# Five conditioning vectors formed behind the expert slots, and the last head group's sum gated a step ahead

## The reference, cut to what matters

```python
mod = (silu(L_c) @ L_wmod).reshape(4, 6, 1, 512)      # one product of 4 x 512 by 512 x 3072
sa, ca, ga, sb, cb, gb = mod[:, 0], ..., mod[:, 5]
ga = sign(ga) * max(|ga|, 0.25);  gb = sign(gb) * max(|gb|, 0.25)
h = layernorm(x) * (1 + ca) + sa
x = x + ga * attn(h)
h = layernorm(x) * (1 + cb) + sb
x = x + gb * ffn(h)
```

## Time and profile before

| | |
|---|---|
| median of 3 runs | 1901.08 us (1898.94 to 1903.13) |
| the profiled execution | 1899.2 us, its span 1897.2 us |
| busy, TensorE (PE) | 1793.4 us, 95% |
| busy, TensorE's weight loads (PEld) | 1402.9 us, 74% |
| busy, VectorE (DVE) | 1179.9 us, 62% |
| busy, ScalarE (ACT) | 753.7 us, 40% |
| busy, GpSimd (POOL) | 682.8 us, 36% |
| DMA | 216.33 MB, 114 GB/s mean |
| chain that ended last | TensorE 76%, VectorE 10%, DMA 5%, GpSimd 3%, ScalarE 2% |

### The profile page before, as it was taken

How to read it: one execution, slowest core, us unless ns; L and a number is a source line. 1 busy time by engine, 2 the same in 40 slices (tenths; PEclk the granted TensorE clock), 3 DMA queues, 4 the chain that set the end, 5 groups by cost and what they waited for, 6 DMA issues and landing times.

```text
span 1897.2 us, 25664 instructions
## 1 busy us (share of the span) xinstructions
PE 1793.4 (95%) x8308; PEld 1402.9 (74%) x8308; DVE 1179.9 (62%) x2156; ACT 753.7 (40%) x1465; POOL 682.8 (36%) x674
## 2 busy tenths in 40 slices
PE   8889999999999999997897999949999999999998
PEld 4556788888888888885664777738778788788786
DVE  4555766666766666767773444466655747567576
ACT  2533455455455554543451222256642122212211
POOL 1334321222121121202153555634565445536332
PEclk9999999999999999999997999969999999999999
DMA  6122253635355454532267899740111011001001
GB/s 249 46 89 86 87 166 103 200 101 191 84 156 154 144 166 129 152 96 98 73 227 267 243 278 270 148 133 12 34 34 50 7 34 50 19 20 50 11 29 72
DMA packets 99953, 216.33 MB, mean 114 GB/s; under 512 B 8504, under 2 KB 33096, under 8 KB 98336
## 3 DMA queue, kind: packets, MB, share of 16 engines
q1 hardware_dynamic: 77744, 166.60, 27.5%
q0 software_dynamic: 11520, 28.96, 6.6%
q10 hardware_dynamic: 10608, 19.74, 3.2%
HBM read 123.93 MB, written 91.35 MB: 113 GB/s over the span
## 4 chain that ended last, share of the span: by engine, by line
PE 76%; DVE 10%; DMA 5%; issue 4%; POOL 3%; ACT 2%; POOLq 0%; ACTq 0%; DVEq 0%; SPq 0%
PE bank L781 21%; PE bank L783 20%; PE bank L782 20%; DMA u_d<-yt,sm 3%; PE bank L1167 3%; PE bank L1022 3%; PE bank L885 2%; PE bank L968 2%; DVE hh L2252 1%; POOL hs_d L2426 1%; DVE rr L1921 1%; PE bank L970 1%; PE bank L826 1%; PE bank L1168 1%; DMA gbt<-mod_rows_d,sm 1%
## 5 line engine op out<-in xcount | busy, mean ns | idle before, releaser
L1921 DVE RECIPROCAL rr<-rr 128x256 f32<-128x256 f32 x128 | 218.8, 1730 | 0.0
L781 PE MATMUL bank<-W1a,hT 128*128 128x512 f32 x512 | 209.9, 410 | 3.4 <-DVE hT L1833 3.4
L781 PE MATMUL bank<-hT,W1b 128*128 128x512 f32 x512 | 208.1, 406 | 2.6 <-DVE hh L2209 2.6
L782 PE MATMUL bank<-hT,W1b 128*128 128x512 f32 x512 | 203.3, 397 | 0.0
L783 PE MATMUL bank<-hT,W1b 128*128 128x512 f32 x512 | 203.2, 397 | 0.0
L783 PE MATMUL bank<-W1a,hT 128*128 128x512 f32 x512 | 201.5, 393 | 0.0
L782 PE MATMUL bank<-W1a,hT 128*128 128x512 f32 x512 | 200.7, 392 | 0.0
L2342 POOL TENSOR_TENSOR x<-x,tmp 128x512 f32<-128x512 f32 x60 | 95.9, 1598 | 245.9 <-DVE tmp L1913 245.9
L2209 DVE TENSOR_TENSOR hh<-hh,bank 128x512 f32<-128x512 f32 x64 | 43.7, 687 | 183.8 <-PE bank L783 147.3
L1946 DVE SCALAR_TENSOR_TENSOR kt<-bank,kt 128x256 fp32r<-128x256 f32 x128 | 50.7, 396 | 162.5 <-ACT vt L1388 162.3
L2276 POOL TENSOR_TENSOR W<-stage,W 128x1024 fp32r<-128x1024 f32 x32 | 77.2, 2412 | 184.4 <-ACT W L1250 182.1
(11 more groups left out here) (280 smaller groups left out, 4468.1 us busy)
## 6 DMA issues: line engine op xcount, KB each, us to landing
hs_d<-bor SPq DMA_DIRECT2D x24, 1548.0 KB, 11.7
ws_d<-W SPq DMA_DIRECT2D x48, 512.0 KB, 6.1
WB<-ws_d SPq DMA_DIRECT2D x8, 3072.0 KB, 18.8
stage<-wa SPq DMA_DIRECT2D x32, 512.0 KB, 5.2
stage<-wbe SPq DMA_DIRECT2D x24, 512.0 KB, 4.2
stage<-wdn SPq DMA_DIRECT2D x24, 512.0 KB, 3.9
mw<-wmod SPq DMA_DIRECT2D x10, 1024.0 KB, 4.9
hg<-hs_d ACTq DMA_DIRECT2D x39, 258.0 KB, 4.7
```

What stands on the lines that cost most here:

```text
L781: pe.matmul(o, lhs(HI), rhs(HI), start=start, stop=False, **kw)
L782: pe.matmul(o, lhs(HI), rhs(LO), start=False, stop=False, **kw)
L1921: dve.reciprocal(rr[:, pair, h], rr[:, pair, h]).then_inc(r_rec, 1)
```

## The change

It has two halves.

**The five late parts.** Five parts of layer 1 (SA, CA, SB, CB, GBT) are taken out of the tables of group 0, and so out of `mod_load`, `mod_products`, `mod_evac` and `mod_out`. They are made behind the expert slots instead:

- SyncE loads their weights (five times 1 MB, into a buffer `lw` of their own) at the end of `slots()`; the second and the fourth load wait for the end of the sixth and the seventh expert.
- TensorE makes the five products and four turns at the start of `back()`, into banks 0, 1, 4, 5 and 7, ahead of the transposes of the layernorm of batch 0.
- ScalarE copies rows and columns (`late_row`, `late_modc`) between and behind its diagonals, ahead of `ln_scaled(2, 0)`. `ln_scaled(2, 1)` goes behind `ln_out((2, 0))`.
- GpSimd makes the gate of GBT, and its transfer to `rows_d`, at the end of `step_c(0)` (`late_gate`).

**The last group's sum.** GpSimd multiplies `x` by the gate row and adds `x0` for a whole batch (`begin_gated`, eight operations), a step ahead of the batch's last tail. The tail is then one VectorE operation, PSUM times `row` into `tmp`, and GpSimd's add of `tmp` to `x`. The loads of `x0` for batches 2 and 3 stand in step (7,2), behind the counts that say where their buffers are free.

```diff
-MOD_PARTS = [(0, GAT), (0, SB), (0, CB), (0, GBT), (1, GAT), (1, SA), (1, CA), (1, SB), (1, CB), (1, GBT)]
-MOD_FINISH = [(0,), (3,), (4,), (9,)]
-MOD_PLACE = [(0, 0), (0, 1), (0, 2), (1, 0), (1, 2), (2, 0), (2, 1), (2, 2), (3, 0), (3, 2)]
+MOD_PARTS = [(0, GAT), (0, SB), (0, CB), (0, GBT), (1, GAT)]
+MOD_FINISH = [(0,), (3,), (4,), ()]
+MOD_PLACE = [(0, 0), (0, 1), (0, 2), (1, 0), (1, 2)]
+LATE_PARTS, LATE_ROW, LATE_BANK = [SA, CA, SB, CB, GBT], [0, 1, 2, 3, 1], [0, 1, 4, 5, 7]
@@ SyncE, called for i = 0 to 4 at the end of slots() @@
+            def late_load(i):
+                if i in (1, 3):
+                    e = (GE - 3, GE - 2)[i // 2]
+                    end = sp.value_load(tab[0:1, TAB_END, e:e + 1], min_val=1, max_val=SLOTS)
+                    sp.wait_ge(w_all, 16 * GE)
+                    sp.wait_ge(dn_full, end)
+                sp.dma_start(lw[:, i, :], wmod1[LATE_PARTS[i]]).then_inc(lw_loaded[i], 16)
@@ SyncE, load_x_again(b) @@
-                    sp.wait_ge(ring_done, RING[("tail", "A", GA - 1, {2: 0, 3: 2}[b])] + NT)
+                    sp.wait_ge(x_pre, NT * (b if b == 3 else 1))
                 sp.dma_start(x0[:, X0_AT[b], :, :], x_in[b].rearrange("(t p) n -> p t n", p=P)) \
@@ TensorE @@
             def back():
+                for i in range(3):
+                    late_product(i)
+                late_columns(0)
+                late_product(3)
+                late_columns(1)
+                late_product(4)
+                late_columns(2)
+                late_columns(3)
                 for half in range(2):
                     ln_transposes((2, 0), half)
@@ ScalarE, back() @@
                     for c in range(NC):
                         act.activation(dg[:, b, HI, c, :], ident[:, :], ACT.Copy, scale=gcol[:, c, b:b + 1]) \
                             .then_inc(dg_hi, 1)
+                    if b < 3:
+                        late_row(b)
+                late_modc(0)
+                late_row(3)
+                late_modc(1)
+                late_row(4)
+                late_modc(2)
+                late_modc(3)
                 ln_scaled(2, 0)
-                ln_scaled(2, 1)
                 ln_out((2, 0), 0)
                 ln_out((2, 0), 1)
+                ln_scaled(2, 1)
@@ VectorE, tail_evac @@
-                if ts == "A":
-
-                    link(dve.tensor_tensor(tmp[:, par, :], TAIL[par][:, :], xt, ALU.add), sum_done, tb * NT + t + 1)
-                    dve.tensor_tensor(tmp[:, par, :], tmp[:, par, :], row[:, tb % 2, :], ALU.mult) \
-                        .then_inc(ring_read, 1)
-                else:
-                    dve.tensor_tensor(tmp[:, par, :], TAIL[par][:, :], row[:, tb % 2, :], ALU.mult) \
-                        .then_inc(ring_read, 1)
+                dve.tensor_tensor(tmp[:, par, :], TAIL[par][:, :], row[:, tb % 2, :], ALU.mult).then_inc(ring_read, 1)
@@ GpSimd @@
+            def begin_gated(b):
+                pool.wait_ge(ring_read, RING[("tail", "A", GA - 2, b)] + NT)
+                pool.wait_ge(row_full[b % 2], 16 * (b // 2 + 1))
+                for t in range(NT):
+                    xt = x[:, b * NT + t, :]
+                    gated = pool.tensor_tensor(xt, xt, row[:, b % 2, :], ALU.mult)
+                    gated.then_inc(x_mul, 1)
+                pool.wait_ge(x_mul, NT * (b + 1))
+                pool.wait_ge(x0_loaded[X0_AT[b]], X0_COUNT[b])
+                for t in range(NT):
+                    xt = x[:, b * NT + t, :]
+                    pool.tensor_tensor(xt, xt, x0[:, X0_AT[b], t, :], ALU.add).then_inc(x_pre, 1)
@@ GpSimd, add_tail @@
-                    if ts == "A":
-                        pool.wait_ge(x0_loaded[X0_AT[tb]], X0_COUNT[tb])
-                        pool.tensor_tensor(xt, x0[:, X0_AT[tb], t, :], tmp[:, (key + t) % 2, :], ALU.add) \
-                            .then_inc(ring_done, 1)
-                        continue
                     pool.tensor_tensor(xt, xt, tmp[:, (key + t) % 2, :], ALU.add).then_inc(ring_done, 1)
@@ GpSimd, called at the end of step_c(0) @@
+            def late_gate():
+                v = prow[:, LATE_ROW[4], :]
+                pool.wait_ge(lm_row, len(LATE_PARTS))
+                gate(v)
+                pool.dma_start(rows_d[R_GB1], v).then_inc(row_stored[R_GB1], 16)
@@ GpSimd, step_a, ahead of the tail @@
+                if last and b > 0:
+                    begin_gated(b)
@@ GpSimd, step_a, at its end @@
+                if last and b == 0:
+                    begin_gated(0)
```

More of the change, by code:

```diff
@@ L437, in build @@
         nw_loaded = sem("norm_w_loaded")
+        lw_loaded = [sem(f"late_part_loaded{i}") for i in range(len(LATE_PARTS))]
+        lm_full = sem("late_part_full")
+        lm_row = sem("late_part_row_copied")
+        lc_full = sem("late_columns_full")
+        lc_done = sem("late_columns_copied")
         gw_loaded = sem("router_weights_loaded")
@@ L663, in step_a @@
                         wa_slice(1, 1)
-                    for i in ((1, 2, 3), (4, 5), (6, 7, 8), (9,))[b]:
+                    for i in ((1, 2, 3), (4,), (), ())[b]:
                         mod_load(i)
@@ L721, in slots @@
                     load_expert(e)
+                for i in range(len(LATE_PARTS)):
+                    late_load(i)
             def back():
```

58 lines of the change are left out of this document (41 added, 17 removed).

## The result

| | before | after | ratio, 95% interval |
|---|---|---|---|
| five runs of either | 1898.94 us (1896.81 to 1903.13) | 1886.62 us (1881.89 to 1888.96) | 0.9929 (0.9916 to 0.9943) |
| the same kernels, a later comparison (`after_again`, 6 runs) | 1900.51 us | 1889.75 us (1882.48 to 1891.17) | 0.9944 (0.993 to 0.9958) |

The change gives 11 to 13 us, where 21 were forecast. The measured 1886.6 lies in the predicted range (1867 to 1890), half a microsecond outside the forecast's own (1872 to 1886), and nearest to the case half way to rival B.

What follows compares the result with a forecast made beforehand. TensorE was taken as the bound, so time could come only where it isn't full or its work can move into idle time. Terms -12.5 - 8.0 - 5.8 + 1.0 - 1.0 + 5.0 = -21.3 gave 1879 us, range 1867 to 1890.

Steps and rivals of the forecast that it cites:

- rival B: Whole kernel: gains shrink, last group gives nothing, late gate costs 8, clock falls in (0,2); -7.7, 1893 us; chance 0.19.
- (0,2): Group 0, step (0,2) without its late products and turns: 47.5 us shortened by 12.5; replay -13.7, or -10.7 if the clock falls.
- (0,3): Group 0, step (0,3): loses two products of 3.6 us and two turns, becomes a step of 25.86 us; -8.0, other end -6.
- transposes to 129, the tail from 129.8: Replay of step (0,2) after the q projections: tail starts at 129.8 instead of 143.34, step ends at 137.0 instead of 150.7.
- The last group: Head group 7: one VectorE operation less per tile; +1.7 in (7,1), -3.3 in (7,2), -3.2 in (7,3), -1.0 behind; sum -5.8.
- The slots: Expert slots: 5 MB of late loads behind the last expert's weights slow TensorE by 1 us, ends 0 and +4.
- At a tenth of loss: Slots term: 17 us more of full DMA load at a tenth of loss is 1.8 us, part fitting into free time.
- Behind the slots: Late products after the last slot: ln_scaled(2,0) 1.4 late, but ln_scaled(2,1) moved behind ln_out(2,0); -1.0, ends -2.5 and +1.5.
- The late gate: End of step_c(0): GpSimd's five gate operations hold VectorE's small operations ahead of the first normed; +5.0, ends 0 and +8.
- the chain is through before the first two-input one: Late gate's end of 0: scalar forms hold nothing, VectorE's small operations finish before GpSimd's first two-input operation.
- C: Rival: products behind the slots run at 1.2 GHz, 35.3 us instead of 17.65; 1900 us, no change; chance 0.05.
- D: Rival: GpSimd's gating falls on VectorE's critical chain in (7,1) to (7,3), up to 31 us; +8, 1909 us; chance 0.04.

Runs made afterwards that it cites:

- tail_first: Against the changed kernel: in steps (0,2) and (0,3) VectorE reads the tail's first tile ahead of its four kvb operations; ratio to before 0.9900.
- paced_loads: Against the changed kernel: the five late weight loads are spread, one every two slots, load i waiting for slot 28 + 2i; ratio to before 0.9918.
- tail_and_pace: Against the changed kernel: tail's first tile ahead of kvb in (0,2) and (0,3), and five late loads spread over slots 28 to 36; 1877.78 us, ratio 0.9890.
- two_input_gate: Against the changed kernel: six unused two-input GpSimd operations replace the gate at the end of step_c(0), the gate moves to step_c(1)'s end; ratio to before 0.9958.
- gated1_behind_tail: Against the changed kernel: begin_gated(1) stands behind the tail of step (7,1), not ahead of it; ratio to before 0.9929.

## Why the prediction was right, and where its terms were off

- **(0,2), -12.5 forecast, -10.0 found; (0,3), -8.0 and -6.2.** The replay was right up to the tail (the third split at 116.12, which is 118.45 less the 2.3 us by which (0,2) began earlier; the wait 2.56 for 2.6). The step that failed is "transposes to 129, the tail from 129.8": it followed TensorE and VectorE, and did not ask when ScalarE's `kvb` is ready. On VectorE the tail's first tile stands behind the operations that wait for it. The product removed had covered that. tail_first shows it: with that order the terms are -12.7 and -7.6.
- **The last group, -5.8 forecast with the -1.0 ahead of the slots.** After's trace has -5.1 in (7,0) to (7,3) and -2.9 ahead of the slots. Over the twelve kernels with the new tail, (7,0) to (7,3) take 137.0 to 139.6 against 142.3 in both with the old one, and the way to the first slot 75.8 to 79.1 against 79.2 in both: -2.6 to -5.3, and 0 to -3.4. The means are -3.8 and -1.8, together -5.6, where the sum has -5.8. The mechanism was right to the operation: four `kvb` of 0.89 to 1.37 in (7,1) and one of 1.40 in (7,2), tail tiles at 0.69. Only (7,1) lost 1.8 and (7,2) gained 4.3 in place of 1.7 and 3.3.
- **The slots, +1 forecast, ends 0 and +4; found +5 to +7.** This is the term that was mis-sized most, and outside its ends. "At a tenth of loss" took the loss for one of TensorE's share beside a busy DMA. What is late is single small gathers beside the loads, most of all beside two at once, and what waits for them is VectorE's queue. A mean over 25 us cannot show that.
- **Behind the slots, -1.0 forecast, found +1.2 to +2.6 with all five loads in bursts and the new order.** The order on ScalarE gave what it should, and ScalarE's copies cost nothing: after's `xw` starts 1.26 us behind its last one, and waits for VectorE's scales. The loss is ahead: the last scatter is issued 4.8 and 3.9 us behind the last slot product in after's two traces, where it was 3.1, and `x` is loaded behind it. In paced_loads it is 2.3, and the first transpose comes 21.9 us behind the slots (before 21.4, after 23.3): of the loss ahead of the transpose, 1.4 of 1.9 us go with the bursts. The first normed came hardly earlier in that trace (55.3, after 55.4), with the clock at 0.50 for 3.4 us longer; tail_and_pace, without that, has 54.0.
- **The late gate, +5.0 forecast, found 0.** The sum took all five operations as holding, from the copy. A scalar form costs 0.4 us where it starts. The other end, 0 by a rule for two-input operations alone, was right, and its ground too: "the chain is through before the first two-input one". two_input_gate shows +4.3 where they are all of that kind. The rule of the Trainium skill ("SBUF — State Buffer", section "Who interferes with whom") that a VectorE instruction with two SBUF inputs and a GpSimd one that reads SBUF exclude each other for the whole instruction agrees with these six, and not with the gate's scalar forms: L2174, two inputs, ran in 0.16 inside one of 1.94. The measurement decides.
- **The rivals.** C (late products at 1.2 GHz) did not come: the first three late products, 24 passes from 1213.53, take 10.46 us, 0.44 a pass. D (the gating on VectorE's critical chain) did not either: begin_gated(2) ended ahead of the layernorm's chain. Its mechanism is real at another place: gated1_behind_tail loses 5 us in (7,2), where the gating meets the constants for the routing. B, the shrunken gains, is nearest to the time, but only its smaller (0,2) and slower slots came, and not its lost tail and its 8 us of gate.

The gate's 5 us, which did not come, and the 5 by which the slots cost more than their term cancel. That is luck. After's trace is 17.1 us shorter than before's, 4.2 short of the sum. Group 0 is 4.3 short, the slots 5.3, the stretch behind them 2.8, and stages that the sum left alone lost 1.5, most of it behind the first normed (0.9). Against that stand the gate's 5.0, the last group with the way to the first slot 2.1, and 2.5 at the start, which is chance.

One thing is open. The profiled executions differ by 17.1 us (after_again's by 16.5), the medians by 12.3 and 10.8, and after's profiled execution is its fastest in both comparisons. So of the 9 to 10.5 us by which the medians are short of the sum, the trace explains 4.2. Where the unprofiled runs of after lose the rest no trace shows.

## What to carry to other kernels

When work is taken out from between two engines, replay every queue up to the next hand-over, and not only the two that waited: the third one had been covered as well. Large loads beside small gathers that are on the path cost more than a mean of the DMA load shows. Spreading them one by one gives back a part (2.5 to 3 us of the 6 to 9 that they cost here), and not all. Gating or other two-input work on GpSimd belongs where VectorE reads PSUM or makes long operations, since it is paid one operation at a time.

## What the runs showed of the hardware

- GpSimd's TENSOR_SCALAR on 4x512 (1.5 to 1.9 us) holds a VectorE operation only at its start: 0.55 and 0.60 instead of 0.17, then none. Its TENSOR_TENSOR on the same tile (six in 8.05 us) lets one VectorE operation through at its end and holds the next, 1.12 to 1.14 us.
- The hold is not for two-input operations of VectorE alone: in gated1_behind_tail its TENSOR_SCALAR on 1x16 took 1.12 beside GpSimd's two-input operations, and the same took 0.16 at 845.40 in after. The Trainium skill ("SBUF — State Buffer", section "Who interferes with whom") says that `tensor_scalar` can enter a mode that uses both port pairs of VectorE, where its operands allow it, and can then contend too; this agrees.
- The same wait of TensorE does not always cost the clock. That for the third split of (0,2), 2.55 to 2.59 us in the ten kernels that have it, was followed by a granted clock of 0.50 to 0.69 over 5 us in three and of 1.00 in seven.
- One 1 MB load at a time in the last ten slots: 241 GB/s moved with TensorE idle for 4.0 of 60 us; two at a time: 219 GB/s and 5.7. A gather of gate rows lands 3.9 to 5.6 us behind its issue with no load under way (before), and up to 8.5 beside the spread loads (paced_loads).
